# Second attention layer: the products with the values of a head pair in one batch of five units instead of three batches

## The reference

```python
qkv = jnp.einsum('bsd,ed->bse', x, W_qkv)
...
q = _rope(q, positions)
k = _rope(k, positions)
scores = jnp.einsum('bhqd,bhkd->bhqk', q, k) / jnp.sqrt(jnp.float32(dk))
causal = jnp.tril(jnp.ones((S, S), dtype=bool))
scores = jnp.where(causal[None, None, :, :], scores, -jnp.inf)
attn = jax.nn.softmax(scores, axis=-1)
out = jnp.einsum('bhqk,bhkd->bhqd', attn, v)
```

## Time and profile before

| | |
|---|---|
| median of 3 runs | 3586.07 us (3584.92 to 3587.94) |
| the profiled execution's own time | 3588.78 us |
| its span (first to last instruction) | 3586.9 us |
| TensorE busy | 3273.3 us (91%) |
| VectorE busy | 1987.1 us (55%) |
| ScalarE busy | 1567.3 us (44%) |
| GpSimd busy | 927.5 us (26%) |
| mean granted TensorE clock | 0.941 |

### The profile page before, as it was taken

The page is one execution under the profiler, slowest core; times in us unless marked ns, Lnnn a source line. Parts: engine busy times, 40 slices in busy tenths (PEclk is TensorE's granted clock), DMA queues, the critical chain, the costliest instruction groups (busy, mean ns, idle before and its releaser), DMA issues.

```text
span 3586.9 us, 58807 instructions
## 1 busy us (share of the span) xinstructions
PE 3273.3 (91%) x20560; PEld 2333.5 (65%) x20560; DVE 1987.1 (55%) x6976; ACT 1567.3 (44%) x3441; POOL 927.5 (26%) x1840
## 2 busy tenths in 40 slices
PE   4999789998899979999899998999889998899978
PEld 3676657765677656776567765677656766567665
DVE  3664565555556465554656546566455554566445
ACT  1444344543454334543445525445253542544424
POOL 0222322222222222222222232222322223222222
PEclk7999899998999989999899998999999998999989
DMA  2000000000000000000000000000000000000000
GB/s 80 30 19 7 6 13 25 19 7 1 19 19 19 7 1 25 19 13 7 1 25 19 13 7 1 31 13 13 6 1 31 19 7 6 13 19 19 7 6 7
DMA packets 31438, 53.75 MB, mean 15 GB/s; under 512 B 3472, under 2 KB 13456, under 8 KB 30864
## 3 DMA queue, kind: packets, MB, share of 16 engines
q1 hardware_dynamic: 31120, 49.64, 4.3%
HBM read 44.91 MB, written 4.72 MB: 14 GB/s over the span
## 4 chain that ended last, share of the span: by engine, by line
PE 79%; DVE 11%; issue 4%; POOL 3%; ACT 2%; PEld 1%; PEldq 1%; SPq 0%; DMA 0%; POOLq 0%; ACTq 0%; DVEq 0%
PE outs L896 14%; PE work L820 7%; PE work L781 7%; PE work L857 6%; PE work L802 6%; PE work L858 5%; PE work L859 5%; PE work L903 4%; PE outs L1007 3%; DVE work L1124 3%; PE work L777 3%; PE work L786 2%; PE work L997 2%; PE work L861 2%; PE work L791 2%
## 5 line engine op out<-in xcount | busy, mean ns | idle before, releaser
L1480 ACT ACTIVATE PR<-work 128x512 f32<-128x512 f32 (+1 forms) x1088 | 640.5, 597 | 580.3 <-PE work L859 477.3
L1124 DVE CUSTOM_DVE_ANT_0 work<-work,KEEPB 128x384 f32<-128x384 f32 (+3 forms) x1536 | 665.5, 480 | 75.5 <-PE work L820 74.1
L1606 POOL TENSOR_SCALAR_AFFINE_SELECT PR<-PR 128x256 f32<-128x256 f32 (+1 forms) x960 | 348.3, 366 | 952.5 <-ACT PR L1480 948.6
L1108 DVE TENSOR_TENSOR BIG<-work,BIG 96x512 fp32r<-96x512 f32 (+1 forms) x455 | 285.4, 629 | 355.0 <-ACT BIG L1375 355.0
L820 PE MATMUL work<-BIG 96*128 96x448 f32 (+9 forms) x1664 | 447.9, 367 | 36.6 <-DVE NMX L1124 15.9
L1596 POOL TENSOR_TENSOR TOK<-AB 128x256 f32<-128x256 f32 (+1 forms) x325 | 219.2, 674 | 877.5 <-DVE AB L1078 854.8
L896 PE MATMUL outs<-PR,ONES 128*32 128x512 f32 (+4 forms) x2304 | 404.5, 458 | 0.0
L857 PE MATMUL work<-BIG 99*128 99x512 f32 (+4 forms) x1152 | 404.5, 351 | 0.0
L820 PEld LDWEIGHTS work<-BIG 96*128 96x128 f32 (+1 forms) x1664 | 285.2, 207 | 174.7 <-issue 91.7
L1077 DVE TENSOR_TENSOR AB<-work,COS 128x256 f32<-128x256 f32 (+2 forms) x357 | 150.0, 420 | 426.9 <-PE work L781 366.3
L858 PE MATMUL work<-BIG 96*128 96x512 f32 (+4 forms) x1152 | 382.4, 332 | 0.0
(11 more groups left out here) (161 smaller groups left out, 5280.9 us busy)
## 6 DMA issues: line engine op xcount, KB each, us to landing
WKW<-w_kw_dram SPq DMA_DIRECT2D x65, 256.0 KB, 2.8
WSEL<-w_sel_dram SPq DMA_DIRECT2D x65, 256.0 KB, 3.0
X<-x_dram SPq DMA_DIRECT2D x9, 512.0 KB, 3.4
out_dram<-X SPq DMA_DIRECT2D x9, 512.0 KB, 2.8
WFC<-w_fc_dram SPq DMA_DIRECT2D x1, 1024.0 KB, 9.9
WFP<-w_ffp_dram SPq DMA_DIRECT2D x1, 1024.0 KB, 11.9
WQKV<-w_qkv_dram SPq DMA_DIRECT2D x1, 768.0 KB, 13.0
WQ<-w_q_dram SPq DMA_DIRECT2D x1, 576.0 KB, 7.4
```

Source lines behind the costliest of these rows:

```text
L1108: read_work(v.tensor_tensor(dst[1], src, dst[0].bitcast(F32), ALU.subtract), use)
L1124: last = v.tensor_tensor_reduce(ps[:, lo:hi], ps[:, lo:hi], KEEPB[:, T - (hi - lo):T], -1.0, -NEG, ALU.add, ALU.min, dst)
L1480: a.activation(PR[0:rows, j % NP, :], ps[0:rows, :], ACT.Exp).then_inc(exp_ready, 1)
L1606: gp.affine_select(blocks, blocks, [[0, len(cols)], [1, P]], ALU.is_ge, 0.0, base=0, channel_multiplier=-1).then_inc(exp_masked, 1)
```

## The change

`PV[1]` becomes one batch of all five units. Its matrix products are those of before, sorted by key block: 512, 384, 256 and 128 columns, two heads each. The end of the accumulation moves from key block 2 to key block 3, which is now the last (`LAST`), and the output is complete with batch 0 (`COMPLETE`).

```diff
-PV = [[(2 * k, 2 * k + 1) for k in range(6)], [(0, 1), (2, 3), (4,)]]
+PV = [[(2 * k, 2 * k + 1) for k in range(6)], [(0, 1, 2, 3, 4)]]
...
-COMPLETE = [{4: [A1, A3], 5: [A2]}, {2: [0]}]
+LAST = [2, 3]
+COMPLETE = [{4: [A1, A3], 5: [A2]}, {0: [0]}]
...
                             last = mm(bank[row:row + 32, j * P:T], v, PR[0:rows, slot, col:col + T - j * P],
-                                      start=(j == 0), stop=(j == 2 or a == A2), skip_group_check=True)
+                                      start=(j == 0), stop=(j == LAST[layer] or a == A2), skip_group_check=True)
```

## The result

The changed kernel takes 3597.62 us (median of 7 runs, 3596.33 to 3599.06), the one before 3586.04 (7 runs, 3581.84 to 3587.94). The ratio is 1.0033, with an interval from 1.0022 to 1.0045: 11.6 us slower, where the forecast had 24. The sign and the places of the waits were right; the size of nearly every term was too large, and what happens ahead of the selection mask was wrong.

A forecast was written before the change was run, and what follows sets the result against it. TensorE was taken to bound it (79% of the chain, VectorE 11%). 0.68 + 0.31 + 0 + 0.49 + 0.24 + 1.26 = 2.98 us a sequence, 23.8 by eight, took 3586.07 to 3610; 8-in-10 range 3588 to 3627.

The forecast's parts named there:

- The sign: Whole kernel: the change makes it slower, 3610 us against 3586.07, with 0.82 for slower.
- the places of the waits: Between merged batches, TensorE waits for VectorE at units 0 and 1 (0.2 to 0.3 us each) and the group transpose.
- The drain's price: At boundaries between a pair's batches on TensorE: merging saves 0.54 us a pair, 34.6 us if all on the path.
- term (1): Pair 1's first batch moves out of TensorE's slack in VectorE's stretch into TensorE's own: +0.68 us a sequence.
- The waits in turns: Behind pairs 1 to 4, merged batches no longer cover waits for VectorE: +0.31, 0, +0.49, +0.24 us.
- The first flag: Turn behind pair 2: VectorE's flag for max 3 at 1.51 us, so unit 0 ends at 1.96 instead of 1.69.
- the second flag: Turn behind pair 2: VectorE's flag for max 4 at 2.28 us, so unit 1 ends at 2.73 instead of 2.46.
- The end: Behind pair 5: pair 7's whole batch comes after GpSimd's last mask, held by the last projection's chain: +1.26 us a sequence.
- a move of the mask as a bound: At the sequence's end: if the last projection's chain moves ahead 0.85 us with the mask, the cost is 0.4; total 3603.
- the rival's cause: Around the first merged batch, the granted clock falls to its lower level in all sequences: 9 us more, 3619; chance 15%.
- 3628: Whole kernel, lower-clock rival's worst case: first merged batches run at that level, all of it on the path; rival's chance 15%.
- 3622: Whole kernel: upper limit in us of the main forecast case, 3595 to 3622, given 67%.

The follow-up runs named there:

- the shorter maxima: Second layer's segment maxima over their last 128 columns only, against the kernel before: 3541.65 us with three batches a pair, 3541.02 with one.
- The runs of the end: Against the kernel before: one batch for all pairs but the last, 3594.5 us; only pairs 6 and 7 in one, 3590.03; only pairs 2 to 6, 3594.67.

## Why the prediction was half right

**The drain's price: right where it can be read.** By the changed kernel a batch is 2.28 us (2.27 forecast), and the shorter maxima show 0.55 for two boundaries (0.54) in the one turn without waits. That there is such a price agrees with the rule of the Trainium skill (TensorEngine Tiling, Tiling Modes, Key Properties: changing the tiling mode drains TensorE). That the tiling mode is its cause is not shown: no run changes the group and keeps the mode.

**The step that failed first: term (1), with "VectorE's own stretch doesn't shrink, since TensorE is not what it waits for".** The term took the border between VectorE's stretch and TensorE's as fixed at 461.76 us, and pair 0's batches as work in slack in both kernels. In the changed kernel the chain of the first sequence goes over to TensorE at 453.13, 6.3 us ahead of the mask, and pair 0's merged batch lies on it:

```profile
453.13 0.77 PE work L862
453.90 0.43 PE work L821 x2
...
454.86 0.85 PE work L837 x4
...
456.56 2.42 PE outs L897 x16
```

The stretch of before wasn't one case either. In four of the eight sequences of its profiled execution the granted clock falls to the lower level some 11 us behind the key copy, for 6.8 us in three of them and 3.4 in one; the earlier trace rows is one of these. There the stretch is 22.9 to 23.0 us (22.1 in the one), elsewhere 21.1 to 21.4. VectorE's timeline right in that window shows why:

```profile
1326.10 0.70 DVE L1124 CUSTOM_DVE_ANT_0 work<-work,KEEPB 128x512 f32<-128x512 f32 x1 [1.24 <-PE work L820]
```

VectorE waits 1.24 us for TensorE, which has pair 0's first batch to do at the lower clock (four instructions that take 1.85 us in the chain, where the same batch of pair 3 takes 0.98). I had the window's row before me and used it only for a cost. In the changed kernel the same window of the third sequence (us, busy by engine, clock, DMA, GB/s) has the lower clock too, but VectorE is busy in 6.86 of 7.00 us instead of 5.60, because pair 0's products now come behind it:

```profile
1323.80:1330.80 7.00, 6.44 (x22) 4.83 (x24) 6.86 (x27) 3.50 (x6) 1.74 (x5) 0.51 0.01 2
1330.80:1333.40 2.60, 2.60 (x20) 1.29 (x17) 2.46 (x10) 0.74 (x2) 0.41 (x1) 1.00 0.00 0
```

From the key copy to the end of pair 1's batches it is now 26.67 us (21.04 + 5.63), before 26.83 (21.99 + 4.84). So in the place of +0.68 stands about -0.17. That is a mean over two cases: against the four sequences of before at the full clock (25.9 to 26.2) the changed kernel (26.5 to 26.9) is some 0.6 longer, against the four with the lower clock (26.9 to 27.9) it is shorter. The nearness of the 0.6 to the forecast's 0.68 is luck, since the run with pair 0 alone shows as long a delay behind the mask (0.9) without the move of pair 1's first batch that the term was made of. How much the lower clock costs the kernel before differs between executions: with pairs 0 and 1 untouched, the stretch was 21.32 in the mean in one experiment (no sequence had the low clock there) and 21.58 in another (three had it). The stretch is so 0.3 to 0.95 us shorter a sequence.

**The waits in turns: right in place, about 0.1 us too dear each.** In the mean over the sequences they come to +0.19, -0.10, +0.38 and +0.08 behind pairs 1 to 4, together 0.55, where the prediction had 0.31, 0, 0.49 and 0.24, together 1.04. The first flag was met exactly (unit 0 ends 1.96 us behind the batch, as worked out); the second flag, the normalisation (done 0.07 earlier) and the short transposes each came a few hundredths sooner than I had added up, and the last batch of a chain of such meetings collects them.

**The end: +0.70 instead of +1.26.** I said that GpSimd's last mask is held by the chain of the last projection, "not by the batches", and this failed too. Measured from the end of pair 5's batches the mask came 18.12 us later before (492.33 to 510.45) and 17.60 now (492.35 to 509.95), 0.52 sooner. The runs of the end take this apart: pair 6's merged batch ends 0.42 later (I had 0.9), and from there the mask comes 0.94 sooner, but only where pair 7 is merged too. TensorE's last piece had stood behind pair 7's first batch of 0.98 us, and that batch has left; so this chain does hold the mask, but the batches hold the chain. What comes behind the mask grew by 1.22, as forecast (1.26). 0.42 - 0.94 + 1.22 is the 0.70. The prediction had a move of the mask as a bound (0.85) and took the other end.

**The clock: it did fall; what it cost the changed kernel is not shown.** All eight sequences now have some 3.4 to 6.8 us at the lower clock some 11 to 15 us behind the key copy, before four. So the rival's cause came true. The lower clock ends at about the start of pair 0's merged batch (456.56 us in the first sequence, 2.42 us long instead of 2.28), so the batch itself runs at the upper level; but the 3.43 us of TensorE's chain ahead of it (453.13 to 456.56) lie in it. No sequence of this kernel is without it for a comparison. Other runs allow one between their own sequences: those in which it covers the merged batch are 1.35 us longer than those in which it mostly lies ahead of it (pairs 0 and 1 merged), and those in which it lies right ahead of the batch are 1.2 to 1.5 us longer than those without it (shorter maxima). The windows on both sides read:

```profile
449.50:456.40 6.90, 5.99 (x20) 4.64 (x20) 6.79 (x27) 3.38 (x7) 1.81 (x5) 0.54 0.00 1
456.40:467.00 10.60, 10.58 (x79) 6.52 (x78) 8.85 (x38) 6.55 (x12) 2.59 (x7) 0.98 0.00 1
```

**The sum.** -0.17 + 0.55 + 0.70 = 1.08 us a sequence, 8.6 by eight, against a difference of the spans of 8.9 and of the medians of 11.6. With the stretch of an execution of before without the low clock (a saving of 0.3) it would be 1.7, so 14: the measured difference lies between. Two bounds of the prediction don't follow from its terms: its 3628 should be 3627 (3610 and 8 x 2.15), and nothing written there leads to 3622, the top of the forecast's own range.

**What the three batches were good for** came out more fully than the prediction had it. The first covers VectorE's maxima (turn 5.72 where it stays, 5.85 where it goes, 5.40 where VectorE is fast), the second the normalisation ahead of the group transpose (6.82 to 7.23 when it goes), the third ScalarE's copies of the transposed maxima (a wait of 0.48 when it goes). No merging tried here beats three batches with the full maxima; those with pairs 0 and 1 merged (1.0006) and with pairs 6 and 7 (1.0007) are the closest, with no measurable difference.

## What to carry to other kernels

A saving per batch is real only if nothing else wanted the time between the batches: list, for each place that a batch leaves, which bank comes free next there and which engine reads it, before the saving is counted. When a stretch is said to be paced by one engine, look at all its repetitions and at the clock of each; at half the clock the slack of the other engine can be gone, and moving work out of it is then a gain. Ask too whether the border of the stretch stays where it is: work pushed late into the slack of an engine can put that engine on the chain before the old border. For a term under 1 us in a loop, compare its own stretch in the traces of several executions, since the untouched rest varies as much.

## What was not expected of the hardware

- A boundary between batches costs 0.27 us of TensorE at the full clock (turn of 5.95 against 5.40 us for two), with no record of idle time for it: it shows as a longer group behind the batch (0.43 against 0.24) and as a merged batch shorter than its three parts (2.28 against 2.53).
- In a kernel whose instructions repeat eight times, the granted clock fell to the lower level some 11 to 15 us behind the key copy in 4 of 8 sequences before, and in 3 and none of 8 in two other kernels whose instructions there are the same (pairs 6 and 7 merged; pairs 2 to 6). In the four kernels with the full maxima and pair 0 merged at its place (all pairs, pairs 0 to 6, pairs 0 and 1, pair 0 alone) it fell in 8 of 8. Each is one profiled execution. One of the two levels, 1.2 or 2.4 GHz, is granted at a time, and the earlier trace rows at 0.52 is nearly all the lower one. TensorE was busy in 7.89 of the 11.2 us ahead of such a fall before, and in 7.90 of 11.3 in the changed kernel. The rows of these windows, of before and of the changed kernel (us, busy by engine, clock, DMA, GB/s):

```profile
1309.60:1320.80 11.20, 7.89 (x32) 5.64 (x32) 9.86 (x42) 4.50 (x9) 0.59 (x2) 0.80 0.01 1
```

```profile
1312.50:1323.80 11.30, 7.90 (x32) 5.64 (x32) 10.00 (x41) 4.51 (x9) 0.66 (x3) 0.80 0.01 1
```

What decides whether it falls was not found.
